# Pacing the indirect gathers of a pairwise-interaction tower: landings for the first ten couples, product counts for the rest

## The chip, the core and the metric

The kernel runs on one core of one Trainium2 chip. The metric is the time of one execution in device microseconds, lower is better. The engines work side by side and meet through semaphores: TensorE (PE; PEld its weight loads), VectorE (DVE), ScalarE (ACT), GpSimd (POOL) and SyncE (SP), which issues plain DMAs. Indirect DMAs (gathers) are issued by GpSimd.

## The reference, cut to what matters

512 rows (b), 40 features, vectors of 64 floats. Each feature has an embedding table of 1,000 to 125,000 rows. All in float32.

```
e[b, f, :] = tbl_f[ids[b, f], :]                           # 40 lookups per row
z[b, (i, j)] = sum over x, y of  e[b, i, x] * param[y, (i, j), x] * e[b, j, y]   # all 780 pairs i < j
h = relu(concat(z, dense_ctx) @ W_top1 + b_top1)           # (796 -> 512)
h = relu(h @ W_top2 + b_top2)                              # (512 -> 256)
out = h @ W_top3                                           # (256 -> 1)
```

## The kernel before, in words

**Halves, couples, units.** The batch is four blocks of 128 rows, in two halves s of two blocks (PER = 2). Features go by couples n = (2n, 2n+1), 20 to a half. For couple n, TensorE turns the gathered rows of both blocks (line 423) into `abank`, and ScalarE copies them to `xT` (line 637). Then the couple is combined with all couples m < n. This work is cut into 200 units, numbered u, 100 for each half: couple n has about n/2 of them. In the first half couple 10 begins with unit 25, couple 14 with 49, couple 15 with 56, couple 18 with 81 and couple 19 with 90; the second half begins with unit 100. Each unit is one pass of TensorE into a PSUM tile `upsum` (three of them), with param's part `w` as one operand and `xT` as the other, and one product by VectorE (lines 615 and 616 for the kind C, line 622 for all others) with `xT` or `emb` into a slot of `prod` (eight slots). What then sums the product depends on the kind, planned by `cut_units`:

- T and C: TensorE with `sel` into `zbank` (line 489). C is the cluster of two neighbouring couples, three of the four tiles (lines 501 to 506).
- S: ScalarE, sixteen pairs of instructions (line 658).
- V: VectorE (line 596).
- H: GpSimd adds the halves of each vector (line 405), VectorE reduces the rest (line 596), H_LAG units after the product. There are 26 such units, the first is unit 116, the next 119, 122, 128, 132, 134, 137, 141, 144, 148, 152.

A matmul in float32 stands in the trace as two matmuls and two weight loads: the six matmuls of a C unit are twelve and twelve, the four of a T unit (line 532) eight and eight.

**Order.** Every engine runs through the units in the same order, written out ahead. Semaphore `multiplied` counts finished products, `u_ready` finished units of TensorE. TensorE turns couple n six units before its first (TURN_BACK; fewer, TURNS_BACK, for the first twelve), waiting for `gathered[s][n]`, and stands there until the couple has landed. The units of the second half begin while the layers of the first are computed between them (line 444).

**Gathers.** A couple is four indirect DMAs: two features by two blocks, 128 rows of 256 bytes each. GpSimd issues all 160 at the start, in the order of halves and couples (line 396), with one wait ahead of them, for the ids. After them it turns to its halvings. Param is loaded by SyncE (line 361), one piece for each couple with units, into three slots; a load waits until TensorE has finished with the slot.

Of the kernel before, what the change touches and what calls it, by code (L numbers as in the profile page):

```python
# [5 lines left out]
U32 = mybir.dt.uint32  # L6
# [15 lines left out]
T_LAG = 3  # L22
S_LAG = 4
V_LAG = 1
H_LAG = 3

GROUP_LAG = 3

# [2 lines left out]

TURN_BACK = 6
TURNS_BACK = [0, 0, 0, 0, 0, 0, 0, 0, 2, 2, 4, 4]

NO_SCALAR = 12

# [104 lines left out]
def pairwise_tower_kernel(nc, dense_ctx, ids, tables, param, W_top1, b_top1, W_top2, b_top2, W_top3, out):  # L141
# [3 lines left out]
    HALVES = 2  # L145
    PER = BB // HALVES
    PB = PER * P
    NC = N // 2
# [5 lines left out]
    units, stretches = cut_units(N, E, BB)  # L154
    NU, NQ = len(units), len(stretches)
# [13 lines left out]
    def members(s, g):  # L169
        t = counts[s][0]  # L170
        return [u for u in range(NU) if units[u]["s"] == s and
                (units[u]["g"] == g if is_turned(u) else g >= t and units[u]["z"] // P == g - t)]
# [25 lines left out]
    def group_end(s, g):  # L198

        if g < counts[s][0]:  # L200
            return max(summed_at[u] for u in members(s, g))
        return max(u + {"S": S_LAG + 5, "V": V_LAG + 3, "H": H_LAG + 3}[units[u]["by"]] for u in members(s, g))

# [15 lines left out]
    for q in range(1, NQ):  # L219
        n = stretches[q]["n"]  # L220
        at = stretches[q]["first"]
        back = TURNS_BACK[q] if q < len(TURNS_BACK) else TURN_BACK
        at -= back
        if n == 0 and stretches[q]["s"] == 1:
            at = stretches[q + 1]["first"] - TURN_BACK - 2
# [44 lines left out]
    for u in range(NU):  # L270
        if units[u]["by"] in "VH":
            reduce_at.setdefault(min(u + (V_LAG if units[u]["by"] == "V" else H_LAG), NU - 1), []).append(u)

    with ExitStack() as ctx:
        def sb(name, shape, dt=F32):
            return ctx.enter_context(nc.sbuf_tensor(name, shape, dt))
# [4 lines left out]
        def sem(name):  # L281
            return ctx.enter_context(nc.semaphore(name))

        WIDE = max(x["w"] + (x["n"] - x["n"] % 2) * P for x in stretches)
        rows_id = sb("rows_id", [P, BB, N], ids.dtype)
        emb = sb("emb", [P, BB, N, E])
# [25 lines left out]
        gathered = [[sem(f"gathered{s}_{n}") for n in range(NC)] for s in range(HALVES)]  # L312
# [6 lines left out]
        multiplied = sem("multiplied")  # L319
# [16 lines left out]
        def slot(u):  # L336
            return prod[:, u % SLOTS, :]
# [47 lines left out]
        @block.gpsimd  # L385
        def _(pool):
            pool.memset(ident[:], 0.0).then_inc(ident_zero, 1)
            pool.wait_ge(ident_zero, 1)
            pool.affine_select(out=ident[:], in_=ident[:], compare_op=ALU.not_equal, fill=1.0, base=0,
                               pattern=[[-1, P]], channel_multiplier=1).then_inc(ident_ready, 1)  # L390
            pool.wait_ge(ids_in, 16)
            for s in range(HALVES):
                for n in range(NC):
                    for f in (2 * n, 2 * n + 1):
                        for c in range(s * PER, (s + 1) * PER):
                            pool.indirect_dma_start(  # L396
                                emb[:, c, f, :], None, tables[f],
                                bass.IndirectOffsetOnAxis(ap=rows_id[:, c, f:f + 1].bitcast(U32), axis=0),
                            ).then_inc(gathered[s][n], 16)
            for u in range(NU):  # L400
                if units[u]["by"] == "H":

                    pool.wait_ge(multiplied, u + 1)
                    p = slot(u).rearrange("p (q h f) -> p q h f", h=2, f=E // 2)
                    pool.tensor_tensor(p[:, :, 0, :], p[:, :, 0, :], p[:, :, 1, :], ALU.add).then_inc(halved, 1)  # L405
# [338 lines left out]
```

## Time and profile before

| | us |
|---|---|
| median of 3 runs | 548.67 (548.06 to 549.01) |
| profiled execution | 548.24 |
| its span, first to last instruction | 546.4 |
| busy: PE, DVE, ACT, POOL | 322.2, 258.1, 255.2, 185.2 |
| mean granted TensorE clock | 0.84 |

The span is from the first instruction to the last; the execution's own time has 1.8 us around it. A line of the page gives busy time, mean duration in ns and the idle time before, with what ended it. "issue" is a wait that no semaphore of the trace explains, "remote" one that ended with a semaphore update whose sender the trace doesn't tell. Ends of matmuls are modelled.

### The profile page before, as it was taken

The numbers are of one execution on the slowest core, as the hardware profiler recorded it, in microseconds if no ns is written. First come the engines' busy times: TensorE is split into PE (matmuls) and PEld (weight loads), VectorE is DVE, ScalarE is ACT, GpSimd is POOL, SyncE is SP. The second block draws the span as 40 slices with busy tenths as digits, with TensorE's granted clock in tenths as the row PEclk, the third lists the DMA queues.
The fourth block names the chain that finished last, engine by engine and source line by source line (L and its number), as shares of the span: only waits on it lengthen the run. The fifth ranks groups of instructions, "written<-read, shape, count | busy, mean of one in ns | idle before, by whom it ended". The sixth has DMA issues, their size and how long they took to land.

```text
span 546.4 us, 7416 instructions
## 1 busy us (share of the span) xinstructions
PE 322.2 (59%) x2318; PEld 165.8 (30%) x2318; DVE 258.1 (47%) x262; ACT 255.2 (47%) x1961; POOL 185.2 (34%) x192
## 2 busy tenths in 40 slices
PE   0402000220003200299999999899779999999988
PEld 0201000000001000155455544454454344444645
DVE  0000000000000000389899988855437999998590
ACT  1000000000002100389999969734687999995632
POOL 6777777777777760000000000000001122232030
PEclk9998555565555755599999999999889999999999
DMA  2221111211112110174324220032124242420000
GB/s 59 46 50 30 26 26 26 55 26 26 26 25 62 26 26 1 39 268 124 125 89 148 88 95 10 11 92 76 46 95 173 95 143 79 172 95 1 1 2 0
DMA packets 12937, 35.60 MB, mean 65 GB/s; under 512 B 4705, under 2 KB 5985, under 8 KB 11618
## 3 DMA queue, kind: packets, MB, share of 16 engines
q1 hardware_dynamic: 7778, 29.88, 16.4%
q0 software_dynamic: 5120, 5.25, 5.0%
q8 instruction: 18, 0.29, 0.2%
q14 instruction: 21, 0.17, 0.1%
HBM read 35.12 MB, written 0.00 MB: 64 GB/s over the span
## 4 chain that ended last, share of the span: by engine, by line
PE 34%; another core or an unknown queue 24%; issue 19%; ACT 13%; DVE 8%; POOL 1%; DMA 1%; DVEq 0%
ACT prod L658 11%; PE upsum L537 9%; PE upsum L532 7%; DVE prod L622 6%; PE zbank L489 6%; PE abank L444 5%; PE abank L423 1%; DVE z L596 1%; POOL emb L396 1%; PE upsum L501 1%; ACT xT L637 1%; PE upsum L505 1%; PE abank L469 1%; PE upsum L573 1%
## 5 line engine op out<-in xcount | busy, mean ns | idle before, releaser
L658 ACT ACTIVATE prod<-prod 128x64 f32<-128x64 f32 x944 | 227.0, 250 | 8.1 <-issue 7.2
L658 ACT ACTIVATION_READ_ACCUMULATOR prod<-prod 128x1 f32 x944 | 185.3, 196 | 7.7 <-issue 7.7
L396 POOL DMA_INDIRECT emb<-tbl,rows_id x160 | 151.5, 947 | 50.2 <-issue 48.5
L622 DVE TENSOR_TENSOR prod<-upsum,emb 128x1024 f32<-128x1024 f32 x98 | 116.8, 1220 | 107.1 <-remote 68.5
L537 PE MATMUL upsum<-w,xT 64*128 64x512 f32 x392 | 106.0, 641 | 102.3 <-issue 59.1
L405 POOL TENSOR_TENSOR prod<-prod 128x512 f32<-128x512 f32 x26 | 32.9, 1271 | 290.4 <-DVE prod L622 290.4
L622 DVE TENSOR_TENSOR prod<-upsum,xT 128x1024 f32<-128x1024 f32 x82 | 97.7, 1219 | 67.2 <-remote 40.0
L637 ACT ACTIVATE xT<-abank 128x256 f32<-128x256 f32 x40 | 15.1, 378 | 220.1 <-remote 129.3
L532 PE MATMUL upsum<-xT,w 64*128 64x256 f32 x656 | 88.3, 397 | 4.9 <-DVE prod L622 2.6
L537 PEld LDWEIGHTS upsum<-w,xT 64*128 64x128 f32 x392 | 33.8, 191 | 140.3 <-issue 81.2
L532 PEld LDWEIGHTS upsum<-xT,w 64*128 64x128 f32 x656 | 60.3, 190 | 35.9 <-issue 16.8
L501 PE MATMUL upsum<-xT,w 64*64 64x256 f32 x40 | 14.1, 436 | 82.3 <-issue 80.5
L615 DVE TENSOR_TENSOR prod<-upsum,xT 128x512 f32<-128x512 f32 x20 | 13.7, 687 | 99.7 <-remote 76.6
L489 PE MATMUL zbank<-prod,sel 128*32 128x256 f32 x776 | 58.7, 396 | 0.5 <-ACT zT L639 0.5
L596 DVE TENSOR_REDUCE z<-prod 128x16 f32<-128x512 f32 (+1 forms) x39 | 33.3, 856 | 0.0
L489 PEld LDWEIGHTS zbank<-prod,sel 128*32 128x32 f32 x776 | 20.3, 110 | 41.2 <-issue 24.9
L444 PE MATMUL abank<-zT,w 128*128 128x256 f32 (+2 forms) x100 | 27.2, 426 | 8.2 <-ACT xT L637 7.7
L423 PE MATMUL abank<-ident,emb 128*128 128x128 f32 x80 | 18.8, 317 | 21.8 <-DMA emb<-tbl,rows_id 16.0
L501 PEld LDWEIGHTS upsum<-xT,w 64*64 64x64 f32 x40 | 4.0, 141 | 89.7 <-issue 89.0
L444 PEld LDWEIGHTS abank<-zT,w 128*128 128x128 f32 (+2 forms) x100 | 20.5, 213 | 16.3 <-ACT xT L637 10.1
L423 PEld LDWEIGHTS abank<-ident,emb 128*128 128x128 f32 x80 | 8.6, 149 | 41.0 <-issue 32.6
L503 PE MATMUL upsum<-xT,w 64*64 64x256 f32 x40 | 14.3, 440 | 0.0
(46 smaller groups left out, 132.0 us busy)
## 6 DMA issues: line engine op xcount, KB each, us to landing
w<-W_top SPq DMA_DIRECT2D x2, 1792.0 KB, 8.2
emb<-tbl,rows_id POOLq DMA_INDIRECT x160
w<-param SPq DMA_DIRECT2D x2, 1248.0 KB
w<-param SPq DMA_DIRECT2D x2, 1152.0 KB
w<-param SPq DMA_DIRECT2D x2, 1120.0 KB
w<-param SPq DMA_DIRECT2D x2, 1024.0 KB
w<-param SPq DMA_DIRECT2D x2, 992.0 KB
w<-param SPq DMA_DIRECT2D x2, 896.0 KB
```

Of the source, the lines that this page charges most:

```text
L396: pool.indirect_dma_start(emb[:, c, f, :], None, tables[f], bass.IndirectOffsetOnAxis(ap=rows_id[:, c, f:f + 1].bitcast(U32), axis=0),).th ...
L405: pool.tensor_tensor(p[:, :, 0, :], p[:, :, 0, :], p[:, :, 1, :], ALU.add).then_inc(halved, 1)
L423: last = pe.transpose(abank[:, c * P:(c + 1) * P], emb[:, s * PER + c, 2 * n:2 * n + 2, :].rearrange("p i e -> p (i e)"), ident[:])
L444: last = pe.matmul(to, w1[0:rows_of(s, g), g, m * P:(m + 1) * P], zT[0:rows_of(s, g), room(s, g), :], start=start and g == groups[0], stop ...
L489: last = pe.matmul(zbank[t * QUAD:(t + 1) * QUAD, 0:PB], sel[:, QUAD - 2 - 2 * d["r"]:2 * QUAD - 2 - 2 * d["r"]], slot(u)[:, t * PB:(t + 1 ...
L501: pe.matmul(t[0:E, 0, 0:PB], ws[hi, 0:E], xT[hi, s, n - 1, :], start=True, stop=True)
L532: last = pe.matmul(upsum[u % U_TILES][:, h, x * PB:(x + 1) * PB], w[rows, x_load % W_SLOTS, base + x * P:base + (x + 1) * P], xT[rows, s, ...
L537: last = pe.matmul(upsum[u % U_TILES][:, h, :], xT[rows, s, n, at:at + P], w[rows, x_load % W_SLOTS, base:base + BANK], start=True, stop=True)
L596: dve.tensor_reduce(z_view(u), v, AX_X, ALU.add).then_inc(reduced_v, 1)
L622: dve.tensor_tensor(to.rearrange("p (h q) -> p h q", h=2), t[:], f.broadcast_to([P, 2, BANK]), ALU.mult).then_inc(multiplied, 1)
L637: act.activation(xT[:, s, m, :], abank[:, 0:PB], ACT.Copy).then_inc(abank_free, 1)
L658: last = act.activation(ring[:, x * E:(x + 1) * E], ring[:, x * E:(x + 1) * E], ACT.Copy, accum_out=z_view(u)[:, x:x + 1])
```

## The change

GpSimd's list becomes a plan. The first ten couples of the first half are gathered one after the other, each behind a wait for the landing of the couple in front of it. Each other couple has a place in GpSimd's list of units, behind a wait for that many products: 20 units before its own first unit (GATHER_AHEAD), and for the first ten couples of the second half at 22 + 6 n. The wait doesn't ask for landings. H_LAG goes from 3 to 4, so VectorE reduces an H unit one unit later. What is gathered, and all else, stays.

The places that come out, with (half, couple): 5 (0,10); 10 (0,11); 16 (0,12); 22 (0,13) and (1,0); 28 (1,1); 29 (0,14); 34 (1,2); 36 (0,15); 40 (1,3); 44 (0,16); 46 (1,4); 52 (0,17) and (1,5); 58 (1,6); 61 (0,18); 64 (1,7); 70 (0,19) and (1,8); 76 (1,9); then 105, 110, 116, 122, 129, 136, 144, 152, 161 and 170 for couples 10 to 19 of the second half.

```
-H_LAG = 3
+H_LAG = 4
+GATHER_FIRST, GATHER_AHEAD, GATHER_OTHER, GATHER_STEP = 10, 20, 22, 6
...
+    gather_at = {}
+    for q in range(NQ):
+        s, n = stretches[q]["s"], stretches[q]["n"]
+        if s == 0 and n >= GATHER_FIRST or s == 1:
+            at = stretches[q]["first"] - GATHER_AHEAD
+            if s == 1 and n < GATHER_FIRST:
+                at = GATHER_OTHER + GATHER_STEP * n
+            assert at <= stretches[q]["first"] - GATHER_AHEAD
+            gather_at.setdefault(max(at, 0), []).append((s, n))
...
-            for s in range(HALVES):
-                for n in range(NC):
-                    for f in (2 * n, 2 * n + 1):
-                        for c in range(s * PER, (s + 1) * PER):
-                            pool.indirect_dma_start(
-                                emb[:, c, f, :], None, tables[f],
-                                bass.IndirectOffsetOnAxis(ap=rows_id[:, c, f:f + 1].bitcast(U32), axis=0),
-                            ).then_inc(gathered[s][n], 16)
+            def gather(s, n):
+                for f in (2 * n, 2 * n + 1):
+                    for c in range(s * PER, (s + 1) * PER):
+                        pool.indirect_dma_start(
+                            emb[:, c, f, :], None, tables[f],
+                            bass.IndirectOffsetOnAxis(ap=rows_id[:, c, f:f + 1].bitcast(U32), axis=0),
+                        ).then_inc(gathered[s][n], 16)
+
+            for n in range(GATHER_FIRST):
+                if n:
+                    pool.wait_ge(gathered[0][n - 1], 16 * 2 * PER)
+                gather(0, n)
             for u in range(NU):
+                for s, n in gather_at.get(u, []):
+                    if u:
+                        pool.wait_ge(multiplied, u)
+                    gather(s, n)
                 if units[u]["by"] == "H":
                     pool.wait_ge(multiplied, u + 1)
```

## Rows read from the trace of the kernel before

**Rows 1.** The page: the span, and busy tenths of two engines in 40 slices.
```profile
span 546.4 us, 7416 instructions
...
DVE  0000000000000000389899988855437999998590
...
POOL 6777777777777760000000000000001122232030
```
**Rows 2.** Windows: length, busy us (instructions) by engine, granted clock, DMA share, GB/s.
```profile
3.20:22.20 19.00, 4.00 (x18) 1.63 (x18) 1.02 (x2) 1.16 (x3) 14.43 (x16) 1.00 0.26 58
22.20:203.30 181.10, 20.23 (x92) 8.05 (x92) 5.92 (x6) 6.43 (x35) 137.09 (x145) 0.61 0.16 33
...
227.70:361.40 133.70, 128.60 (x1086) 67.36 (x1090) 118.73 (x112) 119.44 (x953) 0.00 (x0) 0.98 0.31 104
```
**Rows 3.** The gathers' line: ns min/median/max, first and last start.
```profile
L396 POOL DMA_INDIRECT emb<-tbl,rows_id x160: 943/947/1100, 3.2 to 202.3; - x160
```
**Rows 4.** Timeline of the first 22 us: start, length, engine, line.
```profile
3.20 1.10 POOL L396 DMA_INDIRECT emb<-tbl,rows_id  x1 [1.73 <-DMA rows_id<-ids]
4.60 0.95 POOL L396 DMA_INDIRECT emb<-tbl,rows_id  x1 [0.30 <-issue]
...
12.11 0.95 POOL L396 DMA_INDIRECT emb<-tbl,rows_id  x1 [0.30 <-issue]
...
14.53 0.69 PE L423 MATMUL abank<-ident,emb 128*128 128x128 f32 x2 [4.21 <-DMA emb<-tbl,rows_id]
...
15.25 0.39 ACT L637 ACTIVATE xT<-abank 128x256 f32<-128x256 f32 x1 [4.51 <-PE abank L423]
...
19.49 0.69 PE L423 MATMUL abank<-ident,emb 128*128 128x128 f32 x2 [1.84 <-DMA emb<-tbl,rows_id]
...
21.79 0.39 ACT L637 ACTIVATE xT<-abank 128x256 f32<-128x256 f32 x1 [6.15 <-remote]
```
**Rows 5.** Timeline from 44 to 228 us, the rows that carry the argument.
```profile
44.21 0.39 ACT L637 ACTIVATE xT<-abank 128x256 f32<-128x256 f32 x1 [22.04 <-remote]
...
46.54 1.27 PEld L532 LDWEIGHTS upsum<-xT,w 64*128 64x128 f32 x8 [0.76 <-issue]
46.54 1.67 PE L532 MATMUL upsum<-xT,w 64*128 64x256 f32 x8
...
77.80 0.69 DVE L615 TENSOR_TENSOR prod<-upsum,xT 128x512 f32<-128x512 f32 x1 [37.97 <-remote]
...
100.20 1.23 DVE L622 TENSOR_TENSOR prod<-upsum,xT 128x1024 f32<-128x1024 f32 x1 [21.38 <-remote]
...
105.80 0.39 ACT L637 ACTIVATE xT<-abank 128x256 f32<-128x256 f32 x1 [61.21 <-issue]
...
173.00 0.39 ACT L637 ACTIVATE xT<-abank 128x256 f32<-128x256 f32 x1 [66.81 <-remote]
...
227.78 0.39 ACT L637 ACTIVATE xT<-abank 128x256 f32<-128x256 f32 x1 [34.30 <-remote]
```
**Rows 6.** Timeline: the last gather, and the products of units 7 and 8.
```profile
202.26 0.95 POOL L396 DMA_INDIRECT emb<-tbl,rows_id  x1 [0.30 <-issue]
...
227.68 2.36 DVE L622 TENSOR_TENSOR prod<-upsum,emb 128x1024 f32<-128x1024 f32 x2 [19.36 <-remote]
```
**Rows 7.** Timeline: second halves of the products of units 100, 130 and 172.
```profile
360.96 0.41 DVE L616 TENSOR_TENSOR prod<-upsum,xT 128x256 f32<-128x256 f32 x1
...
431.59 0.42 DVE L616 TENSOR_TENSOR prod<-upsum,xT 128x256 f32<-128x256 f32 x1
...
487.68 0.42 DVE L616 TENSOR_TENSOR prod<-upsum,xT 128x256 f32<-128x256 f32 x1
```
**Rows 8.** The halvings' and the products' lines: ns min/median/max, first and last start.
```profile
L405 POOL TENSOR_TENSOR prod<-prod x26: 1255/1272/1283, 408.7 to 525.2; 128x512 f32<-128x512 f32 x26
...
L622 DVE TENSOR_TENSOR prod<-upsum,emb x98: 1214/1218/1226, 117.0 to 523.8; 128x1024 f32<-128x1024 f32 x98
```

## The prediction

> **What bounds the kernel now.** The page first [rows 1]: in the first 16 or so of the 40 slices GpSimd is busy and everything else all but idle, from slice 17 on the other engines are near full. So there are two kernels in a row. The table by stretch [rows 2] puts the border at 227.7 us: before it VectorE works 1.0 us in one stretch and 5.9 us in the 181 us of the next; in the 133.7 us after it, 118.7.
>
> GpSimd issues 160 gathers without a pause, 0.947 us each and 0.30 us between [rows 3], one in 1.25 us, the last at 202.26 us [rows 6]. That is slow, but it isn't what holds the others: the eighth gather, couple 1's last, starts at 12.11 us and TensorE turns the couple at 14.53 [rows 4]. So a gather is landed and seen some 2.4 us after its start. Couple 19 of the first half would be there at about 105 us, yet ScalarE fills that half's sixth xT tile at 173.00 and the seventh at 227.78 [rows 5].
>
> What is late is told by VectorE's and TensorE's rows [rows 5]. From about 22 us on TensorE's "done" reaches others long after its work: its eight matmuls at 46.54 (1.67 us, with eight weight loads) release a product at 100.20. Count instructions between two releases: 12 loads and 12 matmuls of a cluster unit from 44.21 to 77.80 us, 8 and 8 to 100.20, 2 and 2 to 105.80. That is 33.6/24, 22.4/16 and 5.6/4: 1.40 us per instruction each time. The work itself, 1.67 us for the sixteen of the second case, is far shorter.
>
> Before 22 us it isn't so: the transposes at 14.53 release ScalarE at 15.25, those at 19.49 at 21.79 [rows 4], about 1.6 us late. And it doesn't end with the gathers: after the last, VectorE waits 19.36 us more, until 227.68 [rows 6]. Then all is fast at once, with VectorE busy 118.7 of 133.7 us [rows 2]. (227.7 - 3.2) / 160 is 1.403 us. I read this as a server that spends 1.40 us on each gather while they are issued every 1.25: its backlog grows by 0.15 us with each, is 24 us at the last, and 203.2 + 24 = 227. While it is well filled, each other engine gets one instruction through per gather. At 19 to 22 us, 13 to 16 gathers in, the backlog is 2.0 to 2.4 us; below about 2 us nothing is held up. What the server is the trace doesn't show.
>
> **The change, part by part.** *The first ten couples.* A couple is four gathers. Its successor now starts when it has landed: three steps of 1.25 us, and 2.5 us from the fourth's start to the next couple (the 2.4 of TensorE's case and a little for the restart) [rows 4], 6.25 us a couple. The server needs 4 x 1.40 = 5.6 of it, so it comes empty each time. GpSimd is through at 3.2 + 9 x 6.25 + 4.7 = 64.2 us. Behind the waiting gather on GpSimd's queue stand only other gathers. The 25 units of these couples need 25 x 1.43 us = 36 us (92 products between the end of product 8, 230.0 us [rows 6], and that of product 100, 361.4 [rows 7], are 1.43 each) and hide between the landings, even if TensorE has less than its full clock there (0.61 granted in the long stretch [rows 2]); the last of them are done at some 75 us.
>
> *The other couples of half 0 and the first ten of half 1.* 80 gathers, released by product counts 5, 10, 16, 22 (two couples), 28, 29, 34 and so on to 76. The first 24 to 32 of them find their counts reached at 64 us or soon after and run back to back; after 14 or so the backlog passes 2 us, the products slow down, and GpSimd goes on until it meets a count that isn't there. Each pause lets the server drain and the others run. From count 22 to 76 there are 68 gathers, 95 us for the server, against 54 units, 77 us at 1.43. So in this stretch the server sets the pace, not the units: 80 x 1.40 = 112 us from 64.2, less the 2 us that may still stand at the end, puts the last of the 80 at about 174 us and product 76 at 169. Every couple is then there well ahead of its transpose, 14 units after its release. No gathers are due until count 105, so 25 units more at 1.43 bring product 100 to 169 + 35.7 = 204.7 us. Before it ended at 361.4 [rows 7].
>
> *The last ten couples of half 1,* counts 105 to 170. 40 gathers, 56 us of the server, in 65 units. Products 130 and 172 end at 432.0 and 488.1 us [rows 7], 1.34 us each, so the 65 take at least 87 us and the server comes empty in between. The gathers share GpSimd with the halvings, 1.272 us each [rows 8]. Where both hang on nearly the same count (116, 122, 144, 152) the halving is done 5.0 + 1.3 = 6.3 us after it, and VectorE wants it after five more products, 6.7 us: just in time with the H_LAG of 4, 0.9 us late with 3. I take 1 us, bounds 0 and 5 (one product missed at each of the four).
>
> *Everything else,* from product 100 to the end: 546.4 - 361.4 = 185.0 us [rows 1, 7], with its waits at the first half's layers, where no gather has a part. The param loads move earlier with their units; each then has some gathers beside it. DMA is busy 0.31 of the time in the stretch with the densest loads [rows 2] and 0.16 by gathers with few loads, so together under half: nothing, with 3 us as the upper bound (ten of 40 couples 0.3 us late).
>
> One rule speaks against the change, and nothing above rests on it. The row of the gathers has a minimum of 943, a median of 947 and a maximum of 1100 ns [rows 3], though VectorE's products at 77.80 and 100.20 us, among others, fell on them [rows 5]. The Trainium skill ("SBUF — State Buffer", section "SBUF: two separate sides") says that descriptors of GpSimd's DMAs can't be written while VectorE holds the port pair that the two share, which it does in a two-port mode. Now the gathers lie beside busy VectorE work. By the rows the sum stays as it is; by the rule it is the fourth case below, worked out there from rows.
>
> **Sum.** 204.7 + 185.0 + 1 = 390.7 us of span. The profiled execution has 548.24 us at 546.4 of span, so 1.8 more: 392.5; the median of the runs shown, 548.67, is 0.4 above that execution. The sum is no finer than its 2 us of threshold, and I say 391.
>
> **The rivals.**
> (1) *The backlog never bites again.* If runs of gathers of this length pass, GpSimd's 1.25 us is the pace: couple 19 of half 0 is the 18th after 64.2, issued at 154 and landed at 156, where unit 84 turns it; 17 more products at 1.43 end at 180. 180 + 185 + 1 + 1.8 = 368. For it: the first 13 gathers ran free. Against it: 18 couples without a pause are five times that. The pace counts also let the engines get only as far as the gathers.
> (2) *Other work uses the same server.* From 227.7 to 361.4 us the four engines pass 3241 instructions [rows 2] in 133.7 us without such steps, so one costs at most 0.041 us of it. At a fifth of that, the 76 units up to the last of the 80 gathers (2600 instructions at that rate) add 21 us: 412. At half they add 53: 444. Then the first ten couples, with 0.6 us to spare each, lag too. Nothing in the trace excludes it, since before the two hardly met.
> (3) *Slower: it is not the backlog but a gather under way that holds the others.* Then the pauses help nobody: 62 us of the first ten couples with 25 units only crawling, 120 gathers x 1.40 = 168 us of standstill, and the 318 us of work from 227.7 us on: 548, and 2.5 us for the landing each time TensorE has to wait for a couple, 550 to 570. It decides as soon as four gathers in a row are enough to start the slow steps. Against it: couple 1 passed TensorE and ScalarE between 14.53 and 15.25 us, ten gathers in [rows 4].
> (4) *VectorE keeps GpSimd from issuing.* If each of the later gathers waited for one product of 1.218 us [rows 8], the 80 would take 2.47 us each, 198 us, the last couple of them would start at 252 us instead of 169, product 100 would end at 288, and the sum is 288 + 186 + 1.8 = 476. The gathers' even length speaks against it [rows 3]. The port rule of the Trainium skill named above is this case; the trace, with one input of each product in PSUM, doesn't bear it out.
>
> **How the numbers follow.** Forecast 0.50 (its own range, 378 to 405, from the bounds 0 to 5 and 0 to 3 us and from a threshold of 1 to 3 us of backlog); rival 1 0.22; rival 2 0.20; rival 3 0.03; rival 4 0.05. The range 360 to 440 holds the first, the second and nearly all of the third; about 0.12 is outside. Runs of this kernel differ by 0.2%, so less than that is no change. Faster 0.96; same 0.01 (rival 3 at its lowest); slower 0.03.
>
> **What the profile after would show.** Right: couples 1 to 9 start 6.2 to 6.3 us apart, the tenth ends at about 64 us, and ScalarE follows each within a microsecond. After 64 us gathers in runs of up to 20 or 30, with waits on VectorE's products between them; idle time of "remote" or "issue" kind on VectorE and ScalarE towards the end of such runs, none after count 76. Product 100 near 204 us, then 185 us more. GpSimd's halvings release their sums in time. The prediction is wrong if the slow steps of 1.40 us are there among the first ten couples (rival 3), if they are nowhere and product 100 ends near 180 (rival 1), if gathers take longer than 0.95 us to issue (rival 4), or if the stretch behind product 100 isn't 185 us.

## The result: 457.9 us, 0.83 of the time before, and 67 us above the forecast

| | before | after |
|---|---|---|
| median of 4 runs each, us | 548.47 (548.06 to 549.01) | 457.89 (453.59 to 463.82) |
| ratio | | 0.832 [0.826, 0.838] |
| profiled execution, its span | 548.24, 546.4 | 463.82, 462.0 |
| end of product 25 | | 104.2 |
| end of product 100 | 361.4 | 265.9 |
| from there to the end | 185.0 | 196.1 |

The ratio leaves out the slowest execution of the changed kernel, 463.82, which is the profiled one; its windows are those below, and where it matters a second trace of the same kernel (span 451.0 us, run e5 below) stands beside it.

The direction was right; the time lies outside the range of 360 to 440. One fact is needed for all that follows: on some chips the kernel before takes 548 us, on others 367 (four series of each kind, the medians of a kind within 0.3% of each other), so every comparison of times below is between kernels on one chip, and the text says which kind it was. Each series met its chip once, so whether the chip itself makes the difference or its state at the time is not shown; "chip" stands for both.

**The page after.** Span, busy us by engine, and the busy tenths that answer to [rows 1]:

```profile
span 462.0 us, 7416 instructions
...
PE 356.3 (77%) x2318; PEld 177.2 (38%) x2318; DVE 259.9 (56%) x262; ACT 255.9 (55%) x1961; POOL 184.8 (40%) x192
...
DVE  0023721464373493547388655327989988895760
...
POOL 5565537344363624624400003104476545522400
PEclk9998867587787978859799999889999999999989
...
GB/s 62 45 51 97 120 221 84 43 119 76 35 99 104 20 112 106 121 17 126 20 11 12 22 100 92 64 23 271 100 152 102 106 106 114 124 1 1 0 2 0
```

VectorE no longer sleeps through the first 16 slices, but from slice 5 to slice 20 its digits go up and down (7 2 1 4 6 4 3 7 3 4 9 3 5 4 7 3) where a free stretch has 8 and 9. TensorE is busy 356.3 us with the same 2318 matmuls that took 322 before. Its granted clock fell where it had idled: in the windows below it is 0.68 in 6 us without a matmul, and 0.50 (1.2 GHz, the lower of its two levels) in the 6 us of work behind them.

**Windows,** columns as in [rows 2]: the chain of ten couples, two pieces out of it, the stretch right behind it, products 25 to 100, its last piece by itself, and product 100 to 130:

```profile
0.00:71.00 71.00, 33.37 (x182) 15.48 (x185) 20.35 (x25) 19.96 (x138) 38.57 (x46) 0.88 0.34 97
...
59.00:65.00 6.00, 0.00 (x0) 0.00 (x0) 1.23 (x1) 0.96 (x9) 0.94 (x1) 0.68 0.96 390
65.00:71.00 6.00, 5.20 (x28) 3.22 (x31) 1.90 (x2) 4.19 (x33) 3.77 (x4) 0.50 0.08 18
...
71.00:97.00 26.00, 18.90 (x98) 7.34 (x91) 7.75 (x9) 7.62 (x61) 11.32 (x12) 0.66 0.26 72
...
104.20:265.90 161.70, 124.57 (x882) 61.66 (x886) 94.25 (x88) 96.25 (x755) 58.59 (x63) 0.84 0.21 63
...
229.00:265.90 36.90, 33.91 (x300) 18.30 (x304) 29.31 (x28) 29.32 (x232) 0.83 (x1) 1.00 0.07 16
...
265.90:336.30 70.40, 60.52 (x370) 32.79 (x372) 39.51 (x42) 44.86 (x339) 20.75 (x21) 0.95 0.36 114
```

From 104.2 to 265.9 us VectorE is busy 94 of 162 us. The last piece of it, from 229 us on, has no gathers (GpSimd 0.83 us busy): VectorE 29.3 of 36.9 us, TensorE 33.9. The loss is where gathers are. In the second trace product 25 ends at 102.4 and product 100 at 259.6 us, with 191.4 us from there to the end.

**The gathers' line and the waits** (total us, times, longest):

```profile
L410 POOL DMA_INDIRECT emb<-tbl,rows_id x160: 938/944/1097, 3.2 to 397.7; - x160
...
POOL emb L410 <- DVE prod L647: 145.5, 19, 46.3
...
POOL emb L410 <- DMA emb<-tbl,rows_id: 20.4, 9, 5.8
...
ACT xT L662 <- remote: 51.6, 6, 18.3
...
DVE prod L647 <- remote: 36.1, 10, 7.2
```

A gather takes 938/944/1097 ns, against 943/947/1100 [rows 3], though most now lie beside a busy VectorE; the one of 1.10 us is the first in both kernels, before any product. GpSimd waits 145.5 us for products, so it isn't the bottleneck. What is left of the old picture are the "remote" releases: 51.6 us in six waits of ScalarE, 36.1 in ten of VectorE.

**Timeline, GpSimd:** starts of couples 1 and 2, then first and last gather of the runs that follow the chain, and the first gather of the couple placed at count 76:

```profile
9.88 0.94 POOL L410 DMA_INDIRECT emb<-tbl,rows_id  x1 [1.80 <-DMA emb<-tbl,rows_id]
...
16.30 0.94 POOL L410 DMA_INDIRECT emb<-tbl,rows_id  x1 [1.74 <-DMA emb<-tbl,rows_id]
...
66.01 0.94 POOL L410 DMA_INDIRECT emb<-tbl,rows_id  x1 [5.83 <-DMA emb<-tbl,rows_id]
...
84.73 0.94 POOL L410 DMA_INDIRECT emb<-tbl,rows_id  x1 [0.30 <-issue]
...
97.12 0.94 POOL L410 DMA_INDIRECT emb<-tbl,rows_id  x1 [11.44 <-DVE prod L647]
...
105.85 0.94 POOL L410 DMA_INDIRECT emb<-tbl,rows_id  x1 [0.30 <-issue]
...
111.40 0.94 POOL L410 DMA_INDIRECT emb<-tbl,rows_id  x1 [4.61 <-DVE prod L647]
...
120.14 0.95 POOL L410 DMA_INDIRECT emb<-tbl,rows_id  x1 [0.30 <-issue]
...
225.15 0.94 POOL L410 DMA_INDIRECT emb<-tbl,rows_id  x1 [3.55 <-DVE prod L647]
```

**Timeline, VectorE, ScalarE and weight loads:** rows from within the first of those runs, the rows that end the runs, and product 100's second half (the row of [rows 7]):

```profile
81.10 1.22 DVE L647 TENSOR_TENSOR prod<-upsum,emb 128x1024 f32<-128x1024 f32 x1 [9.56 <-issue]
...
86.00 0.28 PEld L557 LDWEIGHTS upsum<-xT,w 64*128 64x128 f32 x1 [1.14 <-issue]
86.70 0.28 PEld L557 LDWEIGHTS upsum<-xT,w 64*128 64x128 f32 x1 [0.42 <-issue]
86.78 1.23 DVE L647 TENSOR_TENSOR prod<-upsum,emb 128x1024 f32<-128x1024 f32 x1 [4.46 <-remote]
...
89.01 0.38 ACT L662 ACTIVATE xT<-abank 128x256 f32<-128x256 f32 x1 [18.29 <-remote]
...
89.17 2.36 DVE L647 TENSOR_TENSOR prod<-upsum,xT 128x1024 f32<-128x1024 f32 x2 [1.16 <-remote]
...
108.61 0.38 ACT L662 ACTIVATE xT<-abank 128x256 f32<-128x256 f32 x1 [6.75 <-remote]
...
108.77 2.35 DVE L647 TENSOR_TENSOR prod<-upsum,xT 128x1024 f32<-128x1024 f32 x2 [4.58 <-remote]
...
122.96 0.69 DVE L640 TENSOR_TENSOR prod<-upsum,xT 128x512 f32<-128x512 f32 x1 [9.48 <-remote]
...
265.53 0.41 DVE L641 TENSOR_TENSOR prod<-upsum,xT 128x256 f32<-128x256 f32 x1
```

Read the two timelines together. The run from 66.01 us is the chain's last couple and three more, 16 gathers: 66.0 + 16 x 1.40 = 88.4, and ScalarE, after 18.29 us of waiting, goes on at 89.01. The next has 8 from 97.12: 108.3, and both resume at 108.61 and 108.77. The next 8 from 111.40: 122.6, VectorE at 122.96. So the 1.40 us of the prediction set the end of each of these runs. But in each of these runs, one of eight gathers as much as one of sixteen, the others stand, although by the prediction's reckoning its backlog would be 1.2 us after eight, under the 2 us that was to be free. The pace within a run isn't the prediction's either: the four matmuls and four weight loads between the products at 81.10 and 86.78 us make 0.71 us each, and TensorE's own rows come 0.70 us apart (86.00, 86.70), two for each 1.40 us and not one.

### The profile page after: what moved, and what is told of

Its sections match the earlier page's. It is cut to its first block, busy times and chain, and to the rows that moved or that the text cites. A ratio compares the mean times of both kernels' runs of the same rounds, so it can differ in the third digit from the quotient of the medians.

```text
span 462.0 us, 7416 instructions
## 1 busy us (share of the span) xinstructions
PE 356.3 (77%) x2318; PEld 177.2 (38%) x2318; DVE 259.9 (56%) x262; ACT 255.9 (55%) x1961; POOL 184.8 (40%) x192
## 3 DMA queue, kind: packets, MB, share of 16 engines
q0 software_dynamic: 5120, 5.25, 5.4%
## 4 chain that ended last, share of the span: by engine, by line
PE 42%; ACT 15%; another core or an unknown queue 11%; DVE 10%; issue 10%; DMA 6%; POOL 6%; DVEq 0%
ACT prod L683 13%; PE upsum L562 13%; DVE prod L647 9%; PE upsum L557 8%; PE zbank L514 7%; PE abank L469 6%; DMA emb<-tbl,rows_id 6%; POOL emb L410 6%; PE abank L448 1%; PE upsum L526 1%; DVE z L621 1%; PE upsum L530 1%; PE abank L494 1%; ACT xT L662 1%
## 5 line engine op out<-in xcount | busy, mean ns | idle before, releaser
L410 POOL DMA_INDIRECT emb<-tbl,rows_id x160 | 151.2, 945 | 207.3 <-DVE prod L647 145.5
L683 ACT ACTIVATION_READ_ACCUMULATOR prod<-prod 128x1 f32 x944 | 178.9, 189 | 4.9 <-issue 4.8
L562 PE MATMUL upsum<-w,xT 64*128 64x512 f32 x392 | 111.7, 666 | 16.8 <-issue 6.7
L557 PE MATMUL upsum<-xT,w 64*128 64x256 f32 x656 | 103.2, 433 | 25.0 <-issue 9.8
L557 PEld LDWEIGHTS upsum<-xT,w 64*128 64x128 f32 x656 | 67.1, 209 | 64.1 <-issue 31.2
L514 PE MATMUL zbank<-prod,sel 128*32 128x256 f32 x776 | 65.6, 426 | 1.4 <-issue 0.8
L562 PEld LDWEIGHTS upsum<-w,xT 64*128 64x128 f32 x392 | 34.9, 198 | 57.3 <-issue 31.5
L514 PEld LDWEIGHTS zbank<-prod,sel 128*32 128x32 f32 x776 | 21.7, 116 | 49.6 <-issue 29.6
L526 PE MATMUL upsum<-xT,w 64*64 64x256 f32 x40 | 14.6, 448 | 2.8 <-ACT xT L662 1.9
L529 PE MATMUL upsum<-xT,w 64*64 64x256 f32 x40 | 14.9, 454 | 1.2 <-issue 1.2
L528 PE MATMUL upsum<-xT,w 64*64 64x256 f32 x40 | 14.7, 451 | 0.8 <-issue 0.8
```

What stands on the lines that cost most here:

```text
L410: pool.indirect_dma_start(emb[:, c, f, :], None, tables[f], bass.IndirectOffsetOnAxis(ap=rows_id[:, c, f:f + 1].bitcast(U32), axis=0),).th ...
L514: last = pe.matmul(zbank[t * QUAD:(t + 1) * QUAD, 0:PB], sel[:, QUAD - 2 - 2 * d["r"]:2 * QUAD - 2 - 2 * d["r"]], slot(u)[:, t * PB:(t + 1 ...
L526: pe.matmul(t[0:E, 0, 0:PB], ws[hi, 0:E], xT[hi, s, n - 1, :], start=True, stop=True)
L557: last = pe.matmul(upsum[u % U_TILES][:, h, x * PB:(x + 1) * PB], w[rows, x_load % W_SLOTS, base + x * P:base + (x + 1) * P], xT[rows, s, ...
L562: last = pe.matmul(upsum[u % U_TILES][:, h, :], xT[rows, s, n, at:at + P], w[rows, x_load % W_SLOTS, base:base + BANK], start=True, stop=True)
L683: last = act.activation(ring[:, x * E:(x + 1) * E], ring[:, x * E:(x + 1) * E], ACT.Copy, accum_out=z_view(u)[:, x:x + 1])
```

## The experiments

Each is given with the kind of chip it met. That couldn't be chosen, so some kernels stand here two or three times.

### First chip, where the kernel before takes 367.39

**Landing waits alone.** The chain stays, all other couples follow at once:

```
-            for u in range(NU):
-                for s, n in gather_at.get(u, []):
-                    if u:
-                        pool.wait_ge(multiplied, u)
-                    gather(s, n)
+            for n in range(GATHER_FIRST, NC):
+                gather(0, n)
+            for n in range(NC):
+                gather(1, n)
+            for u in range(NU):
```

> The first part of the change alone: the first ten couples each wait for the landing of the one before, and the other 120 gathers follow in one run with no wait for products. H_LAG is 4. Theory A (the one of the prediction: a backlog above 2 us holds the others up, their own instructions cost the server nothing): the run starts at 66 us, slow steps begin some 14 gathers later at 83 us and last until 66 + 120 x 1.40 = 234 us; some 20 products are done by then, 180 are left at the pace of before: about 540 us. Theory B (formed after the result: from the first gather of a run on, the other engines' instructions go through one per gather; only what fits a buffer of some tens of instructions hides it, and it ends 1.40 us per gather after the run's start): the same end at 234 us, slow steps from 75 us, about 540 us too. Both say that this part alone is worth under 10 of the 90 us. Rival C: the landings are what matters, then it is near 458 us.

382.9 us, ratio 1.042 [1.039, 1.045]. Product 25 ends at 87.8, product 100 at 193.4. There were no slow steps at all, with 160 gathers as in the kernel before. The forecasts were for a chip of 548 us and are not tested by this.

**Product counts alone.** The chain's wait goes, the first 40 gathers run freely:

```
             for n in range(GATHER_FIRST):
-                if n:
-                    pool.wait_ge(gathered[0][n - 1], 16 * 2 * PER)
                 gather(0, n)
```

> The second part alone: the first 40 gathers are issued without a pause, the other 120 by product counts as in the changed kernel. Theory A: the backlog of 40 gathers is 6 us, slow steps from 22 us until 3.2 + 40 x 1.40 = 59 us; then 25 units at 1.43 us are done at about 97 us, where the changed kernel was at 104: 450 us. Theory B: the same 59 us for the run, then as in the changed kernel: 450 us. Rival C (the waits for landings are what the gain comes from): above 500 us.

371.32 us, 1.009 [1.005, 1.013]. Product 25 at 75.3, product 100 at 180.9, and 188.2 us from there to the end of the span, 3.2 more than the 185.0 of the kernel before on a chip of 548. The prediction's term for "gathers beside halvings, and H_LAG" was 1 us with bounds 0 and 5. But gathers beside halvings are not what the 3.2 us show: with the landing waits alone, where the last gather starts at 219.8 us and the first halving at 240.8, the same stretch takes 187.8 us, and the four traces of product counts alone have 186.3 to 189.7. Against the landing waits alone, product 25 is 12.5 us earlier: that is what the chain costs. It also shows that the prediction's "done at some 75 us" for the chain's units is the time without the chain; with it they are done at 87.8 even where there are no slow steps.

**Sixty-four rows a gather,** in the kernel before: half of the lookups are left out, and the other partitions of `emb` are filled with a constant.

```
-                                emb[:, c, f, :], None, tables[f],
-                                bass.IndirectOffsetOnAxis(ap=rows_id[:, c, f:f + 1].bitcast(U32), axis=0),
+                                emb[0:E, c, f, :], None, tables[f],
+                                bass.IndirectOffsetOnAxis(ap=rows_id[0:E, c, f:f + 1].bitcast(U32), axis=0),
```

> The kernel before, where each of the 160 gathers fetches 64 rows instead of 128 (partitions 0 to 63; the other 64 partitions of the embeddings hold a constant, written by VectorE in the first 10 us, so half of the lookups are left out). If the server's 1.40 us are a cost per row or byte, they become 0.70, below the 1.25 us between gathers: no slow steps, the work starts at once and follows the gathers, couple 19 landed at 105 us, total near 360 us. If they are a cost per gather, all stays: 545 us.

367.73 us, a gather 0.90 us instead of 0.94; no change of the whole. On this chip nothing could be told of the server, since it didn't show.

**One gather at a time.** The chain stays; each later gather has a count of its own, 1.3 products apart:

```
-GATHER_FIRST, GATHER_AHEAD, GATHER_OTHER, GATHER_STEP = 10, 20, 22, 6
+GATHER_FIRST, GATHER_AT, GATHER_EVERY = 10, 4, 1.3
...
+        at = min(int(GATHER_AT + GATHER_EVERY * k), stretches[s * NC + n]["first"] - 8)
+        gather_at.setdefault(at, []).append((s, n, f, c))
```

> The changed kernel, where each single gather of the later 120 waits for its own product count, 4 + 1.3 k for the k-th, instead of four or eight at one count. At 1.43 us a product that is one gather in 1.86 us. Theory A: no backlog ever forms, so only the first ten couples cost: 368 to 375 us. Theory B: each gather holds the others for 1.40 us, but the buffer takes up what they do meanwhile and the 0.46 us between must empty it; if that suffices, 375 us, if it doesn't, the time stays between 400 and 440, in any case well under the changed kernel's 458. Rival D (a gather costs the others a fixed standstill wherever it lies, and spacing is of no use): 458 us.

382.31 us, 1.039 [1.034, 1.043], the same as the landing waits alone. Products 25 to 100 take 105.7 us here (and 105.6 with product counts alone): the yardstick for this stretch without slow steps, gathers and param loads beside it.

### Second chip, where the kernel before takes 547.88

**The change again, and H_LAG alone undone** (`H_LAG = 3` in the changed kernel).

> The changed kernel itself, unaltered, once more beside the kernel before. The last four kernels ran on a chip on which the kernel before takes 367 us, not 548, and shows no slow steps. Two theories of what the result of 0.83 was. Theory S (the slow steps belong to the chip or its state at the time, not to the kernel): where the kernel before takes about 367 us the changed kernel is slower than it, since the ten waits for landings cost ten times 1.3 us less what was hidden anyway; with product 25 at 87 us instead of 75 it takes 379 to 383 us, a ratio near 1.04. Where the kernel before takes about 548 us it takes 454 to 464, a ratio of 0.83. Theory K (the kernel has the slow steps by itself and the 367 us were luck of a few executions): the kernel before shows both times within one series.

> The changed kernel with H_LAG back at 3, so VectorE reduces an H unit after four more products instead of five. The halving of a unit at 116, 122, 144 and 152 stands behind a couple of gathers of nearly the same count and is ready 6.3 us after it, where four products are 5.3 us: VectorE waits up to 1 us at each of the four, 0 to 4 us more than the changed kernel on the same chip. Rival: the waits are absorbed, since the product after a late reduction starts at once: no difference.

453.81 (445.9 to 454.84) and 454.46 us (443.84 to 456.08), 0.83 of 547.88 both, as in the first measurement. These scatter by 2 to 3%, the kernel before by 0.2%, and the fastest execution of each is 445.9 and 443.84, 0.81, so what H_LAG is worth in time drowns. The two traces show this much: with 3 VectorE waits twice for a halving, 1.8 us in all, with 4 never.

### Third chip, where the kernel before takes 367.77

Three kernels of the first chip again, and a new one.

> The kernel with single gathers at counts 4 + 1.3 k, once more. So far the kernel before takes 548 us on one chip with the changed one at 454, and 367 us on another, where this kernel took 382. If this chip is one of 548 us: theory B (while the server has gathers, each other engine gets one instruction through per gather, and a buffer of some tens of instructions hides the first) says 385 to 420, since a single gather is over before the buffer is full; rival D (each gather costs the others its 1.40 us wherever it lies) says 450 to 460. If it is one of 367 us, 382 again.

> The second part alone (first 40 gathers without a pause, the others by counts), once more. On a chip where the kernel before takes 548 us: theory B says that the run of 40 blocks until 3.2 + 56 = 59 us, and from then on all goes as in the changed kernel, whose product 25 ends at 102 to 104 us: 445 to 455. If the waits for landings were what the gain comes from, above 500. On a chip where it takes 367 us, 371 again.

> The kernel before with 64 rows in each gather instead of 128 (half of the lookups left out, a constant in their place), once more. On a chip where the kernel before takes 548 us: if the server's 1.40 us go by rows or bytes, they are 0.70, less than the time between two gathers, and the kernel takes 366 to 380; if they go by gathers, or by packets (each gather makes 32 in either case), 548. On one where it takes 367 us, 368 again.

383.41 us, 1.045 [1.037, 1.052]; 371.28, 1.008 [1.004, 1.013]; 362.59 (a single execution). The first two repeat the first chip.

**Hold.** The kernel before, TensorE behind the landing of the very last gather, so that no unit runs beside a gather:

```
+            pe.wait_ge(gathered[HALVES - 1][NC - 1], 16 * 2 * PER)
```

> The kernel before, but TensorE starts only when the last of the 160 gathers has landed, at 204.5 us. Nothing else runs before. On a chip of 548 us: if the backlog is one of the gathers alone, it stands at 24 us then all the same and the slow steps last until 227 us, with some products made meanwhile out of the buffer; the 8 products that were made before are now missing: 550 to 562. If the backlog is made of the other engines' instructions, there is none at 204.5 and all is fast from there: 204.5 + 12 + 318 + 2, 536. On a chip of 367 us: 536 as well.

547.44 us, where 536 was expected on this kind of chip: the work behind the release was put 11 us too short. VectorE, rows of its timeline:

```profile
208.74 0.69 DVE L616 TENSOR_TENSOR prod<-upsum,xT 128x512 f32<-128x512 f32 x1 [207.59 <-PE upsum L507]
...
211.91 1.23 DVE L623 TENSOR_TENSOR prod<-upsum,xT 128x1024 f32<-128x1024 f32 x1 [2.14 <-PE upsum L533]
```

VectorE has its first product 4 us after TensorE's release (204.4), and the second follows at once. It is read against the same kernel on a chip of 548, below.

### Fourth chip, where the kernel before takes 549.42

> Single gathers at counts 4 + 1.3 k, a third time, since both times before the chip was one of 367 us. On a chip of 548 us: theory B 385 to 420, rival D 450 to 460. On one of 367 us, 383 again.

The single gathers at last beside a kernel before of the other kind: 403.15 us, 0.734 [0.732, 0.736]. The changed kernel has 0.832, so the spacing of the gathers is worth 12% (0.734/0.832), with what comes with it: the order of the couples and their places change too. "One at a time" is the plan, not quite what GpSimd does: between products 25 and 100 its 58 gathers come as 15 by themselves, 5 pairs and 11 threes, where the changed kernel has six runs of eight and three of four. The time is in theory B's range, and rival D is out. Windows from product 25 to 100, of this kernel here and of the same kernel on the first chip:

```profile
101.50:215.50 114.00, 103.78 (x884) 53.10 (x886) 93.63 (x89) 93.90 (x753) 54.70 (x58) 1.00 0.29 88
```

```profile
86.90:192.60 105.70, 101.69 (x884) 53.65 (x886) 93.64 (x90) 93.87 (x755) 57.99 (x62) 1.00 0.32 96
```

114.0 us against 105.7, with the clock at 1.00, where the changed kernel takes 161.7 with 0.84. The run of 16 gathers from 66 us is still in it, and still holds the others up to 88.7 us, so product 25 ends at 101.5 as it did in the changed kernel (104.2). From product 100 on it is 186.7 us, against 196.1 (191.4 in the second trace).

> The kernel before with 64 rows in each gather (half of the lookups left out), a third time for the same reason. On a chip of 548 us: 366 to 380 if the server's cost goes by rows or bytes, 548 if it goes by gathers or packets. On one of 367 us, 363 to 368 again.

Sixty-four rows again, here 549.52 us, the time of the kernel before. Rows of VectorE's timeline, with half the rows in every gather:

```profile
212.59 0.69 DVE L618 TENSOR_TENSOR prod<-upsum,xT 128x512 f32<-128x512 f32 x1 [37.98 <-remote]
...
227.41 2.36 DVE L625 TENSOR_TENSOR prod<-upsum,emb 128x1024 f32<-128x1024 f32 x2 [13.79 <-remote]
```

The standstill ends at 227.41 us, as with 128 rows (227.68) [rows 6]. The 1.40 us belong to the gather as such, not to its rows or bytes. The number of DMA packets is the same in both, 5120 or 32 a gather, so a price per packet is not excluded.

### Fifth chip, where the kernel before takes 548.3

**One at a time without the chain** (the landing wait removed as in product counts alone), and **one at a time, later and closer** (`10, 12, 1.25`, the chain kept), which empties the run behind the chain.

> Single gathers at counts 4 + 1.3 k, and the ten waits for landings taken out: the first 40 gathers run without a pause. On a chip of 548 us: the run blocks the others until 3.2 + 40 x 1.40 = 59 us with 2 or 3 products made; 23 more at 1.43 us put product 25 at about 93 to 97 us, where the same kernel with the chain had it at 101.5, and what follows is unchanged: 393 to 398 us, 0.72 of the kernel before. If the chain of landings is needed there: above 403. On a chip of 367 us: as the counts alone, 371.

> The chain of the first ten couples kept, and single gathers at 12 + 1.25 k instead of 4 + 1.3 k, so that no run of 16 gathers follows the chain. On a chip of 548 us: that run held the others from 74 to 88.7 us; without it product 25 ends near 90 us instead of 101.5: 390 to 396 us. Rival: a couple is now released 3 to 5 products before its transpose and TensorE waits for it, which gives the gain back: 403. On a chip of 367 us: 382, or some us more if TensorE waits.

401.07 us, 0.733 [0.730, 0.736], and 403.98, 0.736 [0.733, 0.739]; expected were 393 to 398 and 390 to 396. Without the chain, products 1 and 2 come only at 39.0 and 60.6 us, the picture of the kernel before, and yet product 25 ends at 97.8, against 101.5 with the chain on the fourth chip: as soon as the 40 free gathers are worked off, the others have all their data and catch up. On this kind of chip the ten landing waits are worth nothing to gathers spaced like this. With the later counts product 25 ends at 91.0, some 10 us earlier as was expected, but 25 to 100 takes 120.7 us (and the stretch behind it 191.1), and the gain is given back. The total is the rival's 403, but not by its mechanism: TensorE's waits for gathers,

```profile
PE abank L446 <- DMA emb<-tbl,rows_id: 30.9, 8, 9.7
```

are no more than with 4 + 1.3 k (33.9 us in eight), and in both kernels all eight lie in the chain; behind product 25 TensorE waits for no gather. What differs in the traces is how the gathers bunch. With 12 + 1.25 k, 32 of the 60 between products 25 and 100 come in runs of four, and such a run holds the others too:

```profile
100.78 0.94 POOL L405 DMA_INDIRECT emb<-tbl,rows_id  x1 [3.73 <-DVE prod L645]
...
106.58 0.39 ACT L660 ACTIVATE xT<-abank 128x256 f32<-128x256 f32 x1 [2.09 <-remote]
```

100.8 + 4 x 1.40 = 106.4. That these runs are the 6.7 us between 114.0 and 120.7 is argued from this, not measured by itself.

> TensorE starts when all 160 gathers have landed, at 204.5 us, once more; on a chip of 367 us it took 547. On a chip of 548 us: if the backlog is one of the gathers alone, slow steps until 227 us, 10 to 20 us more than on the other chip: 557 to 567. If it is one of the other engines' instructions among the gathers, nothing is left over at 204.5 us: 547 to 549 again.

565.09 us (557 to 567 expected). The timeline of the three engines:

```profile
204.65 0.66 PE L424 MATMUL abank<-ident,emb 128*128 128x128 f32 x2 [204.65 <-DMA emb<-tbl,rows_id]
205.35 0.39 ACT L638 ACTIVATE xT<-abank 128x256 f32<-128x256 f32 x1 [203.33 <-issue]
...
206.57 0.39 ACT L638 ACTIVATE xT<-abank 128x256 f32<-128x256 f32 x1 [0.84 <-issue]
...
208.91 0.69 PE L424 MATMUL abank<-ident,emb 128*128 128x128 f32 x2
...
223.19 0.69 DVE L616 TENSOR_TENSOR prod<-upsum,xT 128x512 f32<-128x512 f32 x1 [222.04 <-remote]
...
227.39 0.39 ACT L638 ACTIVATE xT<-abank 128x256 f32<-128x256 f32 x1 [20.43 <-remote]
```

and windows of some 23 us from 204.6 on, here and then on the third chip:

```profile
204.60:227.40 22.80, 3.91 (x18) 1.63 (x18) 1.02 (x2) 0.78 (x3) 0.00 (x0) 1.00 0.04 12
```

```profile
204.60:227.70 23.10, 20.16 (x108) 8.29 (x107) 8.63 (x11) 6.12 (x38) 0.00 (x0) 1.00 0.24 66
```

TensorE sees the last gather landed at 204.65 here and at 204.37 there. Then, with no gather under way and none to be issued, and with no work having run beside them, this chip passes 18 matmuls in 22.8 us and the other 108 in 23.1; the standstill ends at 3.2 + 160 x 1.40 = 227.2. The whole differs by 17.7 us. So the backlog is the gathers' own, it needs no other instructions, and here it stands between an engine's finished work and the others' knowledge of it, not in the landing: TensorE has done unit 0 and its third transposes by 209.6 us, VectorE hears of unit 0 at 223.19 and ScalarE of the transposes at 227.39.

One thing more is in these rows. The first two pairs of transposes reach ScalarE 0.7 us after their start, with 22.6 us of backlog standing by the prediction's reckoning (227.2 - 204.6). So a backlog far above 2 us lets the first eight of TensorE's instructions through at once, and holds up what comes behind them.

### Two more chips, where the kernel before takes 367.68 and 367.21

> The second part alone (first 40 gathers without a pause, then couples by counts, no waits for landings), a third time, both earlier ones having met chips of 367 us. On a chip of 548 us: with single gathers the waits for landings turned out to be worth nothing (401 without, 403 with them), so 450 to 458 here too, the changed kernel's own time. If couples need the chain: above 465.

> The first part alone (chain of ten couples, the other 120 gathers in one run), a second time. On a chip of 548 us: slow steps from 74 us until 66 + 120 x 1.40 = 234 us; some 16 products before, the other 184 after: 234 + 318 - 12 + 2 = 542, so this part alone is worth 1%. On one of 367 us: 383 again.

> The second part alone once more, for a chip of 548 us. There: 450 to 458 if the waits for landings are worth nothing, above 465 if they are part of the gain. On a chip of 367 us: 371 again.

The parts of the change once more: 371.98 us, 1.013 [1.010, 1.015]; 381.5, 1.038 [1.031, 1.046]; 371.17, 1.009 [1.005, 1.013]. Neither part alone was thus ever seen on a chip of 548, and their forecasts for it stay untested.

## Why the prediction was wrong, point by point

**What held.** The diagnosis: slow steps that end when a server of 1.40 us a gather is through, and that drain by themselves in a pause. The three runs shown end at their start + 1.40 us for each gather, and holding TensorE gave 227.4 against 227.2 worked out. The chain, for nine couples: 6.4 to 6.9 us apart instead of 6.25, and ScalarE's tiles within 1 us of the landings. The fourth case (VectorE blocks the issue) was rightly put low: gathers as short as before. From 229.7 to 275.8 us, between two gathers, 27 products take 46.1 us; the same ones took 45.7 in the kernel before.

**Where the time went.** In the trace the count of 76 products is reached at 225 us (the gather behind it starts at 225.15) instead of 169, the 25 units behind it take 41 us instead of 35.7, and the rest 196.1 instead of 186: 56 + 5 + 10, the 71 us between the trace and the sum. (The second trace has 49 + 6 + 5.) The 56 can be laid out with the prediction's own 1.40 us: the chain's last couple starts at 66.0 instead of 59.5; it and the 76 gathers behind it take the server 112 us, as forecast; and between the runs of gathers the server stands idle ten times, 47 us in all, where the forecast has no pause. 66 + 112 + 47 = 225.

**The step that failed** is the one in the middle: "below about 2 us nothing is held up", and from it "in this stretch the server sets the pace, not the units", which set 75 units under the server's 112 us as if the two overlapped. They do so only in part. While a run of four, eight or sixteen gathers is worked off, the others soon stand; they do their units in the pauses. Since GpSimd waits for their products before it issues the next run, what isn't done meanwhile is added. From product 25 to product 77 (104.2 to 229.7 us) there are 125.5 us. GpSimd's 58.59 us in the window are 62 gathers of 0.944, 87 us of the server; 52 units at the yardstick's 105.7/75 are 73. Side by side that would be 87 us, one after the other 160; it came out halfway. Over the whole stretch the changed kernel needs 161.7 us, 56 more than the yardstick. A part comes through the clock: the same 882 matmuls took TensorE 124.6 us at 0.84, and 103.8 at 1.00 with the gathers spaced out. How much of those 21 us lay on the path was not measured.

Two smaller terms of the sum were wrong as well. The chain's units were to be done at some 75 us; they need until 87.8 even on a chip without slow steps, and were done at 104.2 here, so the counts from 22 on were late and the run behind the chain stopped at 16 gathers instead of 24 to 32. And loads beside gathers were put at nothing, with 3 us as the bound, because DMA would be under half busy. From 59 to 65 us it is 0.96 busy, at 390 GB/s, with the top layers' weights, which SyncE issues at 55.6 to 56.6 us; the ninth couple, in flight then, let the tenth start 10.5 us behind it instead of 6.25.

How it could have been seen: the "2 us" was read from the first 22 us [rows 4], where the others had next to nothing to do: 18 matmuls, the two halves of one product and 3 activations in 19 us [rows 2]. That it is no threshold of backlog, the held kernel shows: its first eight instructions pass at once with 22.6 us standing. A small store of instructions that may be ahead, which idle engines don't fill and busy ones soon do, is the reading that I would put in its place. It fits the held kernel and the hold-ups that begin some five gathers into the run at 66 us and two into the one at 111.4, but it is argued: no run measured the store's size, and the pace of 0.70 us within a run is not explained by it.

**The second half.** Product 100 to the end took 196.1 us (191.4 in the second trace) instead of 186. Gathers one at a time bring it to 186.7; on chips without slow steps it is 186.3 to 189.7 with gathers in fours. So most of the excess is the same failed step, 40 gathers in fours that were counted as free because the server "comes empty in between".

**The range.** The second case, that other work shares the server, gave 412 to 444 and came nearest with its time, but its mechanism is not borne out. If other work used up the server's time, a run with work beside it would end late: while the run from 66 us is worked off, 180 instructions of the four engines pass, 3.7 us at half the price of 0.041 us and 1.5 at a fifth of it. It ends 0.6 us late, the one from 111.4 us with 161 instructions 0.4. The held kernel's backlog stands with nothing beside it at all. The case that was missing is that gathers and units overlap only in part.

**The other half of the truth.** The trace of one chip couldn't tell that the stall is there on some chips and not on others. Where it is absent the change has nothing to remove. Its parts alone give 1.04 (landing waits) and 1.01 (counts); the changed kernel itself never met such a chip, and about 1.04 is inferred, not measured.

**Open.** What the server is, and why some chips lack it; whether the recording of the trace has a part in it (every execution here has a recorded span and clock, so none tells); whether its 1.40 us go by gathers or by something each gather does once whatever its rows; the size of the store; the value of H_LAG; the parts alone on a chip of 548.

## What to carry to other kernels

When two kinds of work share something, ask how far they overlap, before taking the larger: where the kernel before takes 548 us, runs of four and eight quick gathers behind one wait stop everybody, and the same gathers 1.3 products apart cost little (458 against 403 us). A threshold read from a stretch in which the engines are idle says nothing of the stretch in which they are busy. And where a trace shows a stall that no instruction accounts for, run the kernel on several chips first: the best versions here, single gathers by product counts with or without the chain, give 0.73 where the kernel before takes 548 us, while counts alone cost 1% where it takes 367; single gathers cost 4% there with the chain, and without it were not run there.

## What the runs showed of the hardware

- The same program takes 548 us on some chips and 367 on others, each met once. The gathers are as long on both (of the landing waits alone at 367 us and of the changed kernel at 548, minimum 938 and median 944 ns), one in 1.25 us.
- On the slower kind, 160 gathers leave a backlog that outlives the last landing by 23 us (204.65 to 227.4), in which TensorE's finished work reaches the other engines late: unit 0, done by 209 us, at 223.19. Half the rows in each gather leave it the same (227.41 us).
- The hold-up ends within 0.6 us of the run's start + 1.40 us for each gather, for runs of 4, 8, 16 and 160 gathers (106.58, 108.61, 89.01 and 227.39 us).
- Beside loads of 390 GB/s a couple of gathers landed late: the next one, which waits for it, started 6.8 us after its last gather (66.01 after 59.24) instead of 2.7 (16.30 after 13.62).
- The rule of the Trainium skill ("SBUF — State Buffer", section "SBUF: two separate sides") on VectorE and GpSimd's descriptors is not tested here, and the prediction's fourth case was no case of it. The page ties the lock to two-port modes and to instructions with two inputs in SBUF, and these products read one input from PSUM. In line with that, the gathers beside products took as long as those beside an idle VectorE (median 944 ns, and 947 before [rows 3]).
